# Lightning attention with a top-8 router on one core: seven block products for the keys, queries and gates of two batches, SiLU and tanh on ScalarE, a new order of work

## The chip, the core and the metric

One core of one Trainium2 chip runs the whole kernel, and it is the only program there. The metric is the device time of one execution in microseconds (us), lower is better.

## The reference, cut to what matters

```
x: (B=4, N=512, H=512) f32; 16 heads of 128; blocks of 64 tokens
xn   = layernorm(x)
qkv  = silu(xn @ w_qkv.T)                 # per head q, k, v of 128 each
per head, blocks scanned in order of time, kv starts at 0:
    o  = (q * q_decay) @ kv + ((q @ k.T) * diag_decay) @ v
    kv = block_decay * kv + (k * k_decay).T @ v
out  = norm_w * rms_norm(o over all 2048 columns)
gate = sigmoid(xn @ w_gate.T)
s    = (gate * out) @ w_out.T
logits = xn @ router_weight.T + router_bias      # 64 experts
scores = softmax(logits); top 8 per token
ffn  = xn * sum(top scores) + sum(top scores * expert_bias rows)
return x + s * silu(ffn)
```

## The kernel before, in words

Five engines work from five instruction lists. `Lane.do` and `Lane.dma` (L65, L74) append to the list of one engine, in the order in which the Python code runs, and an engine plays its list strictly in that order, waiting for semaphores where it must (`play`, L84). All DMAs go through the list of one engine, SyncE (`sp`), so a DMA that waits holds back all DMAs behind it. Buffers are handed out in turn by small rings (`Ring`, L100): `ring` for four PSUM banks `psR`, `tring` for the scratch rows `T`, `xring` for six rows `xs`, `rring` for two buffers `raw` of weights.

Products are computed in fp32r with each operand split in a high and a low part: ScalarE copies the high part (`xh`, `wh`, `qh`, ...), VectorE subtracts it to get the low part (`xl`, `wl`, `ql`, ...), and three matmuls (high x high, high x low, low x high) stand for one product.

Work goes in steps of one pair of heads and one batch, 32 of them (`order`), batches 0 and 1 through all eight pairs, then batches 2 and 3 back through the pairs; each step has two heads, so there are 64 units u. For each unit:

- `project` (L311) computes keys, then queries, then gates, each as one group of 12 matmuls of 512 columns (four parts of the inner 512, times three) into a bank of `psR`. `silu` (L329) takes the sigmoid on ScalarE and multiplies on VectorE, and splits the result. `gate` (L475) takes a sigmoid on ScalarE.
- `values` (L349) computes the values of both heads for two tiles of tokens, 24 matmuls of 256 columns, twice a step.
- `scores` (L369) transposes the keys and multiplies keys with queries; `decayed` (L385) weighs them with a table `D` of decays (loaded from `dtab`, which the kernel builds in DRAM at the start); `state` (L416) makes the key-value state after the first half of the tokens, and `mix` (L427) sums the head's output in `psO`.
- `gated` (L445) multiplies `psO`, norm weights and gates, splits the result into `zh`, `zl`, squares `psO` on ScalarE and adds the squares on GpSimd into `ss`.
- `project_out` (L518), once a step, multiplies by the output weights, four tiles of six matmuls, and VectorE adds each tile to `yacc`.

`split_piece` (L286) prepares the weights, each a copy on ScalarE and a subtraction on VectorE. The router (L591 to L668) is spread over the units by a table of due times (`later`, `hook`). At the start, the tiles of `x` are normalised (`moments`, `spread`, `normalise`) in a staggered order, so that VectorE works on one tile while GpSimd takes the root for another, then transposed (`turn`) and split (`place`). At the end, `fetch` (L524) has loaded the rows of all last tiles before they are needed (into `xs`, `raw` and `D`), and `finish_tile`, `scale_tile` and `finish_scaled_tile` scale, multiply and store them, part of it on ScalarE and GpSimd.

Of the kernel before, what the change touches and what calls it, by code (L numbers as in the profile page):

```python
# [13 lines left out]
P = 128  # L14
# [6 lines left out]
NX = 6  # L21
TAKEN = -3e38
# [6 lines left out]
QK = (QK0, QK1)  # L29

# [82 lines left out]
def build(nc, x, w, slope, norm_w, rw, rb, eb, ident_in, steps_in, out):  # L113
    gscr = nc.dram_tensor("gscr", (B * N, H), F32, kind="Internal").ap()
    dscr = nc.dram_tensor("dscr", (NH, ROW), F32, kind="Internal").ap()
    dtab = nc.dram_tensor("dtab", (NH, P, N), F32, kind="Internal").ap()

    with ExitStack() as ctx:
# [7 lines left out]
        xh, xl = sb("xh", [P, 3, KT, N], F32R), sb("xl", [P, 3, KT, N], F32R)  # L126
        wh, wl = sb("wh", [P, 5, 1024], F32R), sb("wl", [P, 5, 1024], F32R)
        vh, vl = sb("vh", [P, 3, 256], F32R), sb("vl", [P, 3, 256], F32R)
        qh, ql = sb("qh", [P, N], F32R), sb("ql", [P, N], F32R)
        kh, kl = sb("kh", [P, 2, P], F32R), sb("kl", [P, 2, P], F32R)  # L130
        ph, pl = sb("ph", [P, 2, C], F32R), sb("pl", [P, 2, C], F32R)
        dh, dl = sb("dh", [P, C], F32R), sb("dl", [P, C], F32R)
        kvh, kvl = sb("kvh", [P, P], F32R), sb("kvl", [P, P], F32R)
        zh, zl = sb("zh", [P, 2, N], F32R), sb("zl", [P, 2, N], F32R)
        rhl = sb("rhl", [P, KT, 2 * E], F32R)
# [3 lines left out]
        qf, kf, vf = sb("qf", [P, N]), sb("kf", [P, N]), sb("vf", [P, 3, 512])  # L139
# [3 lines left out]
        T = sb("T", [P, 4, N])  # L143
        D = sb("D", [P, 2, 2, N])
        sg = sb("sg", [P, 2, N])
        yacc = sb("yacc", [P, 2, 4, H])
        ss = sb("ss", [P, 2, N])
        sq = sb("sq", [P, 2, N])
# [28 lines left out]
        psR = ctx.enter_context(nc.psum_tensor("psR", [P, 4, 512], F32))  # L177
# [14 lines left out]
        ring = Ring(4)  # L192
        tring = Ring(4)
        xring = Ring(NX)
        rring = Ring(2)
        sqring = Ring(2)
# [4 lines left out]
        def mm(o, l, r, start, stop):  # L201
            return lambda e: e.matmul(o, l, r, start=start, stop=stop)  # L202

        def group(o, ops, after, then={}):

            for i, (l, r) in enumerate(ops):
                ev = pe.do(mm(o, l, r, i == 0, i == len(ops) - 1), *(after if i == 0 else ()), *then.get(i, ()),
                           mark=i == len(ops) - 1)
            return ev


        ln_ev = {}
# [5 lines left out]
        def moments(tt, i, ld):  # L218
            return dve.do(lambda v: v.bn_stats(st[:, tt % 4, :], xs[:, i, :]), ld)

        def spread(tt, e):
# [4 lines left out]

        def stat(tt, i, ld):
            spread(tt, moments(tt, i, ld))

        def normalise(tt, i, ld):  # L230
            return dve.do(lambda v: v.tensor_scalar(xs[:, i, :], xs[:, i, :], mv[:, tt, 0:1], rstd[:, tt:tt + 1],
                                                    ALU.subtract, ALU.mult), ld, ln_ev[tt])

        x_ready, x_hi, x_used = {}, {}, {}

        def turn(i, nx, in_psO=False):
            bank, free = (None, o_free[0]) if in_psO else ring.take()
            dst = psO if in_psO else psR[:, bank, :]
            for k in range(KT):
                ev = pe.do(lambda e, k=k: e.transpose(dst[:, k * P:(k + 1) * P], xs[:, i, k * P:(k + 1) * P],  # L240
                                                      ident[:, :]), *((nx, ident_ev) + free if k == 0 else ()),
                           mark=k == KT - 1)
            xring.give(i, ev)
            return bank, ev

        def place(tt, bank, ev, slot, prev_use=None):
            t = tt % 4
            src = (psO[:, :] if bank is None else psR[:, bank, :]).rearrange("p (k t) -> p k t", k=KT)
            dh, dl = xh[:, slot, :, t * P:(t + 1) * P], xl[:, slot, :, t * P:(t + 1) * P]
            hi = act.do(lambda a: a.activation(dh, src, ACT.Copy), ev, prev_use)  # L250
            lo = dve.do(lambda v: v.tensor_sub(dl, src, f32(dh)), hi)  # L251
            if bank is None:
                o_free[0] = (lo,)
            else:
                ring.give(bank, lo)
            x_ready[slot] = x_ready[(slot, t)] = lo
            x_hi[(slot, t)] = hi

        def xpose(tt, i, nx, slot, prev_use=None):
            place(tt, *turn(i, nx), slot, prev_use)  # L260


        seq = list(range(PAIRS)) + list(range(PAIRS - 2, -1, -1))
        to_load = [(0, p) for p in (VV, QK0, GG, QK1, OO)]
        to_load += [(wi, p) for wi in range(1, len(seq)) for p in (VV, QK0, GG, QK1, OO)]
        w_ready, w_hi, w_used, loaded = {}, {}, {}, {}

        def load_piece():
            if to_load:
                wi, piece = to_load.pop(0)  # L270
                i, free = rring.take()
                loaded[(wi, piece)] = i, sp.dma(raw_port[i], raw[:, i, :], w[seq[wi], piece], *free)

        def split_half(wi, piece, c):

            i, ld = loaded[(wi, piece)]
            cs = slice(c * 512, c * 512 + 512)
            w_hi[(piece, c)] = hi = act.do(lambda e: e.activation(wh[:, piece, cs], raw[:, i, cs], ACT.Copy),  # L278
# [3 lines left out]
            if c == 1:  # L282
                rring.give(i, lo)
                load_piece()
# [689 lines left out]
```

How the kernel before makes its waits and increments, by code:

```python
    def play(self, eng):  # L84
        for waits, make, inc in self.queue:
            for sem, v in waits:
                eng.wait_ge(sem, v)
            ins = make(eng)
            if inc:
                ins.then_inc(*inc)
# [836 lines left out]
            @block.sync  # L927
            def _(e):
                sp.play(e)
                for port in xs_port + [dscr_port]:
                    e.wait_ge(port.sem, port.count)
                for lane, v, _ in ends:
                    e.wait_ge(lane.sem, v)
```

## Time and profile before

| | |
|---|---|
| time, median of 2 runs | 1157.47 us (1156.66 to 1158.28) |
| span of the profiled execution | 1155.8 us |
| the profiled runs' time around that span | 1.7 us (median less span) |
| TensorE busy | 1139.6 us, 99% |
| VectorE busy | 782.3 us, 68% |
| ScalarE busy | 521.8 us, 45% |
| GpSimd busy | 103.4 us, 9% |

The page shows one profiled execution. The last row of the table of engines that matters for the result is that of TensorE. Busy matmuls overlap in the records: what one matmul costs is read from the time between two starts, not from its mean duration.

### The profile page before, as it was taken

The numbers are of one execution on the slowest core, as the hardware profiler recorded it, in microseconds if no ns is written. First come the engines' busy times: TensorE is split into PE (matmuls) and PEld (weight loads), VectorE is DVE, ScalarE is ACT, GpSimd is POOL, SyncE is SP. The second block draws the span as 40 slices with busy tenths as digits, with TensorE's granted clock in tenths as the row PEclk, the third lists the DMA queues.
The fourth block names the chain that finished last, engine by engine and source line by source line (L and its number), as shares of the span: only waits on it lengthen the run. The fifth ranks groups of instructions, "written<-read, shape, count | busy, mean of one in ns | idle before, by whom it ended". The sixth has DMA issues, their size and how long they took to land.

```text
span 1155.8 us, 16461 instructions
## 1 busy us (share of the span) xinstructions
PE 1139.6 (99%) x6668; PEld 1005.5 (87%) x6668; DVE 782.3 (68%) x1504; ACT 521.8 (45%) x1132; POOL 103.4 (9%) x97
## 2 busy tenths in 40 slices
PE   8899999999999999999999999999999999999997
PEld 6788888888888888888988888888888888888885
DVE  7565676766767778657576777667676676665557
ACT  4444454444544444544334444445444454444442
POOL 4000000000010001000100000000000000000012
PEclk9899999999999999999999999999999999999999
DMA  5621122112122121111222122112111221111303
GB/s 163 206 69 37 38 64 74 55 46 73 38 73 64 56 83 64 47 55 57 72 71 94 55 67 71 46 51 69 64 46 47 73 64 56 46 37 57 126 19 110
DMA packets 34044, 78.12 MB, mean 68 GB/s; under 512 B 3744, under 2 KB 8112, under 8 KB 33968
## 3 DMA queue, kind: packets, MB, share of 16 engines
q1 hardware_dynamic: 33968, 77.07, 20.3%
q8 instruction: 52, 0.85, 0.3%
q14 instruction: 24, 0.20, 0.1%
HBM read 68.64 MB, written 12.61 MB: 70 GB/s over the span
## 4 chain that ended last, share of the span: by engine, by line
PE 96%; DMA 2%; DVE 1%; ACT 0%; SPq 0%; issue 0%; POOL 0%; DVEq 0%; ACTq 0%
PE psR L202 76%; PE psS L202 9%; PE psO L202 9%; PE psS L373 1%; DMA dtab<-dscr 1%; PE psR L240 0%; DMA xs<-x 0%; DMA D<-dtab 0%; DMA dscr<-dval 0%; DVE wl L281 0%; DVE xl L251 0%; DVE yacc L584 0%; SPq L76 0%; PE psR L608 0%; PE psR L648 0%; DVE yacc L560 0%
## 5 line engine op out<-in xcount | busy, mean ns | idle before, releaser
L332 ACT ACTIVATE T<-psR 128x512 f32<-128x512 f32 x192 | 114.4, 596 | 291.1 <-PE psR L202 290.7
L202 PE MATMUL psR<-xh,wh 128*128 128x512 f32 x768 | 220.1, 408 | 0.4 <-DVE wl L281 0.4
L202 PE MATMUL psR<-xl,wh 128*128 128x512 f32 x768 | 206.6, 391 | 0.0
L202 PE MATMUL psR<-xh,wl 128*128 128x512 f32 x768 | 205.9, 390 | 0.0
L202 PEld LDWEIGHTS psR<-xl,wh 128*128 128x128 f32 x768 | 144.7, 188 | 31.9
L202 PEld LDWEIGHTS psR<-xh,wl 128*128 128x128 f32 x768 | 144.2, 188 | 31.4
L471 POOL TENSOR_TENSOR ss<-ss,sq 128x512 f32<-128x512 f32 x59 | 76.3, 1293 | 860.7 <-ACT sq L463 860.7
L202 PEld LDWEIGHTS psR<-xh,wh 128*128 128x128 f32 x768 | 134.6, 190 | 20.6 <-DVE wl L281 0.6
L281 DVE TENSOR_TENSOR wl<-raw,wh 128x512 fp32r<-128x512 f32 x150 | 114.6, 804 | 32.8 <-ACT wh L278 32.6
L333 DVE TENSOR_TENSOR qf<-psR,T 128x512 f32<-128x512 f32 x64 | 44.3, 692 | 113.8 <-ACT T L332 113.7
L514 DVE TENSOR_TENSOR yacc<-psR,yacc 128x512 f32<-128x512 f32 x109 | 73.1, 689 | 41.5 <-PE psR L202 41.5
L202 PE MATMUL psR<-wh,zh 128*128 128x512 f32 x256 | 100.0, 391 | 0.3 <-DVE zl L454 0.3
L202 PE MATMUL psR<-wh,zl 128*128 128x512 f32 x256 | 99.6, 389 | 0.0
L202 PE MATMUL psR<-wl,zh 128*128 128x512 f32 x256 | 99.6, 389 | 0.0
L333 DVE TENSOR_TENSOR vf<-psR,T 128x512 f32<-128x512 f32 x64 | 43.8, 686 | 71.9 <-ACT T L332 71.9
L278 ACT ACTIVATE wh<-raw 128x512 fp32r<-128x512 f32 x150 | 85.7, 622 | 8.6 <-DMA raw<-w 8.6
L202 PE MATMUL psR<-wh,xh 128*128 128x256 f32 x512 | 83.9, 286 | 0.0
L202 PE MATMUL psR<-wh,xl 128*128 128x256 f32 x512 | 82.5, 283 | 0.0
L202 PE MATMUL psR<-wl,xh 128*128 128x256 f32 x512 | 82.4, 283 | 0.0
L202 PEld LDWEIGHTS psR<-wh,xl 128*128 128x128 f32 x512 | 70.8, 192 | 0.0
L202 PEld LDWEIGHTS psR<-wl,xh 128*128 128x128 f32 x512 | 70.8, 192 | 0.0
L202 PEld LDWEIGHTS psR<-wh,xh 128*128 128x128 f32 x512 | 70.4, 191 | 0.0
(141 smaller groups left out, 1941.8 us busy)
## 6 DMA issues: line engine op xcount, KB each, us to landing
raw<-w SPq DMA_DIRECT2D x75, 512.0 KB, 3.6
xs<-x SPq DMA_DIRECT2D x45, 256.0 KB, 3.9
D<-dtab SPq DMA_DIRECT2D x15, 512.0 KB, 4.8
gscr<-xs SPq DMA_DIRECT2D x16, 256.0 KB, 2.0
out_dram<-yacc SPq DMA_DIRECT2D x16, 256.0 KB, 2.0
dtab<-dscr SPq DMA_DIRECT2D x2, 1792.0 KB
xs<-gscr SPq DMA_DIRECT2D x13, 256.0 KB, 3.9
dtab<-dscr SPq DMA_DIRECT2D x2, 256.0 KB
```

The source lines that it names most:

```text
L202: return lambda e: e.matmul(o, l, r, start=start, stop=stop)
L278: w_hi[(piece, c)] = hi = act.do(lambda e: e.activation(wh[:, piece, cs], raw[:, i, cs], ACT.Copy), ld, w_used.get(piece))
L281: lambda e: e.tensor_sub(wl[:, piece, cs], raw[:, i, cs], f32(wh[:, piece, cs])), hi)
L332: e = act.do(lambda a: a.activation(T[:, t, :], psR[:, bank, :], ACT.Sigmoid), ev, *free)
L333: e = dve.do(lambda v: v.tensor_mul(dst, psR[:, bank, :], T[:, t, :]), e)
L373: turned = pe.do(lambda e, t=t: e.transpose(psS[:, 1024 + t * P:1024 + t * P + P], kf[:, t * P:t * P + P], ident[:, :]), *((ready["k"], *k ...
L471: a = lane.do(lambda g: g.tensor_add(ss[:, y, :], ss[:, y, :], sq[:, j, :]), q, ss_ev.get(y))
L514: e = dve.do(lambda v: v.tensor_add(acc, psR[:, bank, :], acc), ev, y_ev.get((y, t)))
```

## The change

Two batches are now computed together. For a pair of batches and one head, keys and queries (or the gates of two heads) are a product of a 2 x 2 block matrix of weights (rows: the two outputs, columns: the two halves of the inner 512) with a 2 x 2 block matrix of activations (rows: halves, columns: the two batches). Eight block products of 6 matmuls (two parts of 256, times three) were needed; `seven` does it with seven, over sums and differences of blocks (`FACTORS`), seven of weights and seven of activations.

- `combine` builds the sums of activations on GpSimd (four subtractions of 256 columns per pair of token tiles); `tile_a` and `tile_b` transpose 14 blocks for two tiles, where 8 were.
- `weights` builds the sums of weights on GpSimd (four operations of 256 columns per piece) and splits seven blocks in four steps; `value_weights` splits six blocks after one GpSimd sum of 512 columns; weights are prepared anew for each of 16 pairs (15 before).
- The results are shared through PSUM: product 1 is copied by ScalarE from its bank to the bank `psB` (`seed`), product 5 by ScalarE to `T` (`s5`), and VectorE adds after product 6 (`u2`) and after product 7 (`c22`). Product 6 waits for `seed`, products 7 and 3 for `u2`, product 4 for `c22`.
- SiLU is one ScalarE instruction (`Silu`), the VectorE products are gone. The gates are `Tanh` of half the input; `gated` adds 1, and half the norm weight is put in by the split. The router takes its exponentials from `Silu`.
- `psR` has three banks (four before), `T` five rows.
- The work of a pair v is ordered by hand: `first_keys`, `heads`, `second_keys`, `gates` (for the next pair), with `opening` and `closing` at either end of each pair of batches. Deferred splits (`owed`, `settle`) are gone. At the start both batches are normalised one tile at a time. At the end, a plain loop fetches and finishes the last eight tiles.

```diff
+ORDER = (1, 5, 6, 2, 7, 3, 4)
+FACTORS = {1: (0, 0), 5: (1, 4), 6: (2, 5), 2: (3, 1), 7: (4, 3), 3: (5, 2), 4: (6, 6)}
...
+        def combine(t, a, na, b, nb):
...
+            e1 = pool.do(lambda g: g.tensor_sub(c1[:, lo], xb[:, lo], xa[:, lo]), na, nb, *ifree)
+            e3 = pool.do(lambda g: g.tensor_sub(c2[:, lo], xb[:, lo], xb[:, hi]), nb, *jfree)
+            e2 = pool.do(lambda g: g.tensor_sub(c1[:, hi], xb[:, hi], c1[:, lo]), e1)
+            e4 = pool.do(lambda g: g.tensor_sub(c2[:, hi], xa[:, hi], c1[:, hi]), e2)
...
+        def product(n, dst, start, after):
+            iw, ix = FACTORS[n]
+            ks = [slice(k * P, (k + 1) * P) for k in range(2)]
+            ops = [(gh[:, iw, ks[k]], xh[:, ix, k, :]) for k in range(2)]
+            ops += [(gh[:, iw, ks[k]], xl[:, ix, k, :]) for k in range(2)]
+            ops += [(gl[:, iw, ks[k]], xh[:, ix, k, :]) for k in range(2)]
...
+        def seven(kind, nx):
...
+            def p6():
+                ev = product(6, psB[:, :], False, (s["seed"],))
+                e, s5 = psR[:, s["e"], :], T[:, s["t5"], :]
+                s["u2"] = dve.do(lambda v: v.tensor_add(e, psB[:, :], s5), ev, s["s5"])
+                next(nx, None)
...
+            def p7():
+                ev = product(7, psB[:, :], False, (s["u2"],))
+                t, free = tring.take()
+                s5 = T[:, s["t5"], :]
+                s["c22"] = dve.do(lambda v: v.tensor_add(T[:, t, :], psB[:, :], s5), ev, *free)
...
+            def p4():
+                ev = product(4, psB[:, :], False, (s["c22"],))
...
+        for t in range(4):
+            normal(t)
+            tile_a(t, rows_of[t][0], norm[t])
+            if t == 1:
+                all_steps(value_weights(0))
         e = pool.do(lambda g: g.tensor_scalar(dexp[:, :], dexp[:, :], sl[:, :], None, ALU.mult), sl_ev, dexp_ev)
         dval_ev = pool.do(lambda g: g.tensor_tensor(dval[:, :], ebase[:, :], dexp[:, :], ALU.pow), e, ebase_ev)
...
+        def second_keys(v, nx, ow):
+            p1, p5, p6, p2, p7, p3, p4 = seven(QK1, nx)
+            p1()
+            p5()
+            next(ow)
+            p6()
+            p2()
+            p7()
+            next(ow)
+            p3()
+            split_keys(0)
+            p4()
+            split_queries(0)
+
+        def gates(v, nx):
+            p1, p5, p6, p2, p7, p3, p4 = seven(GG, nx)
+            p1()
+            p5()
+            p6()
+            do_scores(v, 2)
+            p2()
+            split_keys(1)
+            p7()
+            split_queries(1)
+            do_state(v, 2)
+            p3()
+            do_mix(v, 2)
+            p4()
+            split_values(1, 1)
...
+        values(0)
+        for t in range(4):
+            normal(4 + t)
+            combine(t, rows_of[t][0], norm[t], rows_of[4 + t][0], norm[4 + t])
+            tile_b(t, rows_of[t][0], rows_of[4 + t][0], norm[4 + t])
...
+            if t == 1:
+                half_values(1, 0)
+                all_steps(weights(QK0, 0))
+        half_values(1, 1)
...
+        opening(0)
+        for v in range(1, 7):
+            steady(v)
+        closing(7, second_rows())
+        values(0)
+        values(1)
+        split_values(0, 0)
+        opening(8)
+        for v in range(9, 15):
+            steady(v)
+        closing(15, nothing())
+        for tt in range(8, 16):
+            fetch(tt)
+            finish_tile(tt // 4 % 2, tt)
```

`finish_tile` is two VectorE operations on a tile and a DMA of it to the output; `fetch` is two loads, of `x` and of `gscr`; `normal(t)` is `stat` (statistics on VectorE, the root on GpSimd) and `normalise`. `steady(v)` is `heads` (which begins with `first_keys`), `second_keys`, `gates`. `closing(15, nothing())` has, after the second keys, scores, state and mix of two units with little between them, and both output products.

## Rows read from the trace of the kernel before

**Rows 1.** The page: busy time of the engines.

```profile
PE 1139.6 (99%) x6668; PEld 1005.5 (87%) x6668; DVE 782.3 (68%) x1504; ACT 521.8 (45%) x1132; POOL 103.4 (9%) x97
```

**Rows 2.** Waits of TensorE (us in total, times, longest us), and two stretches: us, busy by engine, granted clock, DMA.

```profile
PE psS L202 <- ACT kt L392: 5.4, 1, 5.4
...
100.00:600.00 500.00, 500.00 (x2944) 443.07 (x2943) 344.07 (x673) 228.54 (x498) 41.62 (x37) 1.00 0.18 60
```

**Rows 3.** The chain that ended last, one piece of it.

```profile
486.64 10.93 PE psR L202 x48
```

**Rows 4.** The costliest groups: busy us, mean ns.

```profile
L202 PE MATMUL psR<-xh,wh 128*128 128x512 f32 x768 | 220.1, 408 | 0.4 <-DVE wl L281 0.4
...
L471 POOL TENSOR_TENSOR ss<-ss,sq 128x512 f32<-128x512 f32 x59 | 76.3, 1293 | 860.7 <-ACT sq L463 860.7
...
L281 DVE TENSOR_TENSOR wl<-raw,wh 128x512 fp32r<-128x512 f32 x150 | 114.6, 804 | 32.8 <-ACT wh L278 32.6
...
L333 DVE TENSOR_TENSOR qf<-psR,T 128x512 f32<-128x512 f32 x64 | 44.3, 692 | 113.8 <-ACT T L332 113.7
...
L278 ACT ACTIVATE wh<-raw 128x512 fp32r<-128x512 f32 x150 | 85.7, 622 | 8.6 <-DMA raw<-w 8.6
```

**Rows 5.** Timeline of a steady stretch, TensorE, ScalarE and VectorE: start us, duration us.

```profile
511.83 0.60 PE L202 MATMUL psS<-vf,kt 128*128 128x128 f32 x4
...
512.03 0.60 ACT L332 ACTIVATE T<-psR 128x512 f32<-128x512 f32 x1 [1.31 <-PE psR L202]
...
512.65 0.69 DVE L333 TENSOR_TENSOR kf<-psR,T 128x512 f32<-128x512 f32 x1 [1.96 <-ACT T L332]
```

**Rows 6.** One operation of VectorE: duration ns least, median, most.

```profile
L281 DVE TENSOR_TENSOR wl<-raw,wh x150: 676/685/1374, 10.3 to 1107.3; 128x512 fp32r<-128x512 f32 x150
```

**Rows 7.** Timeline of the start.

```profile
3.53 1.31 DVE L219 BATCH_NORM_STATS2 st<-xs 128x6 f32<-128x512 f32 x2 [2.15 <-DMA xs<-x]
...
7.12 0.56 POOL L224 TENSOR_TENSOR rstd<-ve,mhalf 128x1 f32<-128x1 f32 x1 [1.36 <-DVE ve L223]
...
7.56 0.53 DVE L231 TENSOR_SCALAR xs<-xs,mv,rstd 128x512 f32<-128x512 f32 x1
...
9.87 0.99 PE L240 MATMUL psR<-ident,xs 128*128 128x128 f32 x4 [0.33 <-DVE xs L231]
...
10.20 5.78 POOL L715 TENSOR_TENSOR dval<-ebase,dexp 128x33 f32<-128x33 f32 x1
...
36.85 1.22 PE L202 MATMUL psS<-vf,kt 128*128 128x128 f32 x4 [5.44 <-ACT kt L392]
37.73 2.05 PE L202 MATMUL psR<-xh,wh 128*128 128x512 f32 x4
...
41.95 1.07 PE L202 MATMUL psR<-xh,wh 128*128 128x512 f32 x4
```

**Rows 8.** DMA issues in 1129 to 1130.9 us: KB each, us to landing.

```profile
out_dram<-yacc SPq DMA_DIRECT2D x1, 256.0 KB, 2.0
xs<-x SPq DMA_DIRECT2D x1, 256.0 KB, 2.9
xs<-gscr SPq DMA_DIRECT2D x1, 256.0 KB, 3.2
```

**Rows 9.** Timeline of the end.

```profile
1130.28 0.43 SPq L76 DMA_DIRECT2D xs<-x  x1
...
1148.46 0.39 PE L202 MATMUL psR<-wh,zl 128*128 128x512 f32 x1
...
1151.09 1.40 DVE L584 SCALAR_TENSOR_TENSOR yacc<-yacc,ro,xs 128x512 f32<-128x512 f32 x2
```

**Rows 10.** Groups of ScalarE and VectorE: a table load, and the two operations that finish a tile.

```profile
L676 ACT ACT_TABLE_LOAD x1 | 1.3, 1283 | 0.7 <-PEq L967 0.7
...
L560 DVE TENSOR_TENSOR yacc<-yacc,xs 128x512 f32<-128x512 f32 x11 | 8.6, 779 | 0.4
...
L558 DVE SCALAR_TENSOR_TENSOR yacc<-yacc,ro,xs 128x512 f32<-128x512 f32 x11 | 8.2, 745 | 1.1 <-POOL ro L492 1.1
```

More of the change, by code:

```diff
@@ L236, in turn @@
[L236 to L244, printed above, removed]
@@ new lines, in tokens @@
+        def tokens(blk, tiles=range(4)):
+            return [xr[(blk // 2, t)] for t in tiles]
+        steady = [p for v in range(1, 7) for p in ((GG, v), (QK0, v), (QK1, v), (VV, v), (OO, v))]
+        first = [(VV, 0), (QK0, 0), (GG, 0), (QK1, 0), (OO, 0)]
+        sequence = []
+        for r in range(2):
+            sequence += [(p, v + 8 * r) for p, v in first + steady]
+            sequence += [(p, 7 + 8 * r) for p in (GG, QK0, QK1, VV, OO)]
+        to_load, loaded = list(sequence), {}
@@ L792, in split_router @@
             j, ld = held.pop("e")
[L793 to L794 removed]
+            e_ready = split(eh[:, :], el[:, :], xs[:, j, :], ld)
             xring.give(j, e_ready)
[L797 to L803 removed]
@@ new lines, in build, with do_scores, do_state, do_mix @@
+        nw_ev = pool.do(lambda g: g.tensor_scalar(nw[:, :], nw[:, :], 0.5, None, ALU.mult), nw_ev)
+        unit = {}
+        def do_scores(v, i):
+            hh, j = divmod(i, 2)
+            k = 2 * v + hh
+            unit[(v, i)] = decayed(k, j, scores(j))
+            if j == 1:
+                load_decay(k + 2)
+        def do_state(v, i):
+            state(*divmod(i, 2), unit[(v, i)])
+        def do_mix(v, i, last=False):
+            hh, j = divmod(i, 2)
+            ev = mix(hh, j, unit.pop((v, i)))
+            gated(hh, j, 2 * (v % 8) + hh, ev, v % 8 == 0 and hh == 0, last)
@@ new lines, in second_rows, with get, put @@
+        def second_rows():
+            for t in range(4):
+                rows_of[8 + t] = None
+            pairs = {}
+            def get(t):
+                pairs[t] = load_rows(8 + t), load_rows(12 + t)
+            def put(t):
+                (a, lda), (b, ldb) = pairs.pop(t)
+                combine(t, a, lda, b, ldb)
+                tile_a(t, a, lda)
+                tile_b(t, a, b, ldb)
+            get(0)
+            all_steps(value_weights(8))
+            yield
+            get(1)
+            put(0)
+            yield
+            all_steps(weights(QK0, 8))
+            get(2)
+            put(1)
+            yield
+            get(3)
+            put(2)
+            yield
+            put(3)
+            yield
```

1032 lines of the change are left out of this document (561 added, 471 removed).

## The prediction

> **What bounds the kernel now.** I read the busy times first: TensorE is at 99%, VectorE at 68%, ScalarE at 45% [rows 1]. A busy matmul row overlaps its neighbours, so that alone proves little. The waits do: in the whole span TensorE's one wait of note is 5.4 us for `kt` at the start, and between 100 and 600 us it is busy for all of 500.00 us at full clock [rows 2]. The kernel is one unbroken stream of matmuls between a start and an end. What one costs is read from the chain: 48 matmuls of 512 columns in 10.93 us, 0.228 each, though their rows say 408 ns [rows 3, 4]. So a matmul left out is worth 0.228 us as long as nothing else becomes late, and a wait that TensorE did not have is paid in full.
>
> **The stream.** Keys, queries and gates are 2304 matmuls of 512 columns (three rows of 768, one of them in [rows 4]): 144 for each of 16 pairs with two batches. With seven products of 6 for eight it is 126, and 2016 in all: 288 x 0.228 = 65.6 us less. Values, scores, state, mix and output stay as they are. Transposes go from 4 blocks per tile to 14 per two tiles, 112 for 64; four small matmuls take at most 0.60 us [rows 5], and less in a stream, so 48 more are about 5 us, bounded by 0 (beside idle time at the start) and 7. Net **-60.5**.
>
> **Busy time of the others.** VectorE loses 192 SiLU products, 132 us by their rows' means (one of them [rows 4]), and gains 96 additions for `u2` and `c22` (66 us) and more weight splits: 48 x (0.42 + 3 x 0.69), with 0.42 as my estimate for half the columns, + 16 x 5 x 0.69 = 175 us against 150 x 0.69 = 103 (0.69 is the median of [rows 6]). With small items it stays near 780. But GpSimd gains 192 sums of 256 columns, 16 of 512 and 32 for x; with half of 1.29 us for a short one [rows 4] that is 125 + 21 + 21 us on top of 103. The subtraction `wl`, both inputs in SBUF, takes 685 ns as a rule and 1374 at worst, and its mean is 804 [rows 4, 6]: it is the worse when GpSimd adds. That is 18 us now; for GpSimd at 270 us I take 50 more, between 0 (they never meet) and 90 (VectorE spends a third of the time in such operations). ScalarE gains 96 copies (58 us) and splits (161 for 93), near 650. VectorE at some 830 and ScalarE at 650 of 1200 bound nothing by themselves. What counts is how late they are when TensorE asks.
>
> **The new waits.** From the end of a group to ScalarE's start is 0.20 us, its operation takes 0.60, VectorE starts 20 ns later and takes 0.69 [rows 5]. A link (product, one operation, product) is thus 0.8 to 0.9, and with the load of weights behind the wait about 1.0 to 1.1 us. What covers it is one product of 6, 1.37 us. The slack of 0.3 us is less than one operation queued in front. I follow a steady pair in program order, with 0.5 to 0.6 us for each operation in a queue:
> - second keys, `seed`: ScalarE first has `zh`, the square, and the split of values left by the mix before. It is done some 0.4 us late.
> - second keys, `u2`: a subtraction for the output weights stands in front on VectorE and meets GpSimd's sums. 0.4 late.
> - gates, `seed`: four copies of the second keys are in front. 0.2 late.
> - gates, mix: `kvl` needs `kvh`, and in front of that on ScalarE stand the result of `c22` (which waits for VectorE behind the decays) and `qh`. The first part of the mix covers 1.1. 1.2 late.
> - first keys, `u2`: behind the five operations of `decayed`. 0.3 late.
>
> Output tiles and values in `heads` cover all that is due there. Sum 2.5 us a pair, bounds 0 (the queues run ahead) and 6 (each of nine links one operation late). For 12 steady pairs **+30**, for the two openings **+8**.
>
> **The turn and the last units.** After pair 7 the second keys end, then the query split is needed at once (result, copy, subtraction: 2.1 us after the last product), the mix of unit 2 waits for scores, decays and two splits (5 us for 5 of work), and unit 3 the same, while 14 transposes per tile pass three banks whose release hangs on VectorE. I count 15 us of idle TensorE, bounds 5 and 25: **+15**. After pair 15 there is no filler, but fewer operations in the queues: 2.1 + 2.4 + 0.6 + 2.2 = **+7**.
>
> **The start.** Before, TensorE runs undisturbed from 41.95 us [rows 7], and until then it has done 48 matmuls of 256 columns, 72 of 512, small ones and 16 transposes, about 23 us of stream: 19 us are lost. After, VectorE's list has per tile: statistics 0.69 and two short ones, the root on GpSimd 0.56, normalise 0.53, transposes 0.99, ScalarE 0.60, subtraction 0.69 [rows 4, 6, 7]; with the hand-overs 4.6 us, one after the other, where before the tiles were staggered. From 3.5 us, with 2 for the value weights, four tiles end at 24. Then GpSimd's list has the power for the decays, 5.78 us [rows 7], in front of the next root: fifth tile normalised at 28.7. Each tile of the second batch takes 7.1 (2.1 for VectorE and root, GpSimd's four sums 2.6, three transposes, copies and subtractions), and 3 for the key weights: 57. With the last values the products begin at 61, after 18 us of stream: 43 lost, **+24**, bounds 10 and 35. The clock is in this: after its 5.4 us of idleness the first four matmuls took 2.05 us where they take 1.07 [rows 7].
>
> **The end.** Before, the last matmul starts at 1148.46, and the span ends 6.9 us after its end [rows 9], since all loads were issued long before. After, the loop puts into SyncE's list: loads of tile 8, store of tile 8 (waits for VectorE), loads of tile 9, and so on; no load can pass the store in front. Per tile: issue of the store and two loads (starts 0.4 to 0.5 apart), the landing of the second 3.2 after its issue [rows 8, 9], 0.75 and 0.69 on VectorE [rows 10]: 0.9 + 3.2 + 1.4 = 5.5 us. The first tile is ready 2.3 after the last matmul, seven more follow, the last store lands after 2.0: 2.3 + 38.5 + 2.0 = 43 for 7, **+36**. Bounds 25 (landing 2.0 only) and 40.
>
> **Sum.** 1155.8 - 60.5 + 30 + 8 + 15 + 7 + 24 + 36 = 1215.3 us of span, with 1.7 around it **1217 us**, 5% slower.
>
> **Rivals.**
> 1. *The links are covered and the stream stays unbroken.* ScalarE had gaps of 1.31 us and VectorE of 1.96 in the steady stretch [rows 5], and in program order their lists may run ahead. Then the 38 us of pairs and openings fall away and 10 of the turn: 1169, within 2% of before, thus not slower. It decides where a pair loses less than 0.4 us (with 1.0 it would be 1184). Against it: the slack of 0.3 us by the numbers above, and lists that put other work in front. Chance 0.14.
> 2. *VectorE as the bound.* GpSimd's sums come right beside the subtractions of the same piece, so they meet more often than by chance; each doubled one stands in front of a link. At 6 us a pair: 1217 + 14 x 3.5 = 1266. For it: 1374 ns [rows 6]. Against: a third of the time only. Chance 0.12.
> 3. *Table loads.* Before there is one, of 1283 ns [rows 10], since all functions lie in one table. If `Silu` and `Tanh` don't, ScalarE goes to and fro twice a pair (keys, gates), four times in an opening, 32 in all: 41 us, near a link each time: 1258. Nothing in this trace shows either function. Chance 0.08. The Trainium skill (ScalarE: Activation LUTs, Table sets: the hidden batching unit) says that functions are loaded as named sets and a switch costs the load and a drain, some 2.66 us; 32 of these would be 85 us and the time 1302. It lists tanh in two sets as a filler and does not list SiLU; the trace's 1283 ns agrees with its figure for the load alone.
> 4. *The ends are cheap too.* If the loads of the last loop get out ahead (they can't by the list) and the start is 10 us better, with rival 1: 1169 - 36 - 10 = 1123, faster. Chance 0.04.
>
> **How the numbers follow.** The forecast has 0.62, with its own range 1190 to 1245. The range that holds 8 in 10 takes in rival 1 and most of 2 and 3: 1168 to 1262. A measurement of this kernel tells about 2% from no change, so same ends at 1181. Faster is rival 4, 0.04; same is rival 1 and the forecast's thin lower edge, 0.16; slower the rest, 0.80.
>
> **What would show it.** Right: TensorE waits for ScalarE's and VectorE's results in every pair, most of all before the products 6 and 7 and in the mix of the gates; VectorE's busy share near 70%, GpSimd's over 20%; `wl`'s successor `gl` well over 0.69 us in the mean; the first product of keys near 61 us; eight stores 5.5 us apart after the last matmul; one table load. Wrong: TensorE busy without gaps in the middle (rival 1), table loads between keys and gates (rival 3), stores at the end closer than 4 us, or 288 matmuls less giving other than 0.228 each.

## The result and the profile after

The changed kernel took 1320.85 us in the median of 2 runs (1320.17 to 1321.53), the kernel before 1157.47: a ratio of 1.141, 95% interval 1.137 to 1.144. It is 14% slower, where 5% was forecast, and above the range. The span of the profiled execution is 1318.4 us.

The busy times, against [rows 1]:

```profile
PE 1142.0 (87%) x6422; PEld 971.1 (74%) x6422; DVE 854.2 (65%) x1527; ACT 637.3 (48%) x1364; POOL 311.2 (24%) x337
```

The records have 246 matmuls less, and TensorE's share falls from 99% to 87%. No other engine has become full. ScalarE's table load stayed the only one, against the same row in [rows 10]:

```profile
L831 ACT ACT_TABLE_LOAD x1 | 1.3, 1283 | 0.7 <-PEq L1238 0.7
```

The waits of TensorE (what is waited for: us in total, times, longest), where [rows 2] had one of 5.4:

```profile
PE psR L215 <- DVE yacc L684: 20.9, 21, 2.3
PE psR L269 <- POOL xs L291: 18.8, 8, 8.6
PE psB L215 <- DVE psR L477: 16.7, 7, 5.1
PE psO L215 <- DVE kvl L601: 16.4, 16, 2.7
PE psR L269 <- DVE yacc L259: 13.6, 3, 5.4
PE psR L269 <- DVE xs L259: 13.1, 3, 6.2
PE psB L215 <- ACT psB L442: 6.8, 4, 3.0
PE psR L215 <- DVE yacc L682: 5.4, 4, 1.5
```

L684 and L682 are VectorE's addition and copy of output tiles, which give banks back; L291 is GpSimd's `combine`; L477 is `u2`; L601 is `kvl`, the low part of the key-value state, which the mix needs; L442 is the seed; the two L259 are the normalisation at the start.

For a table by stage I count, for each matmul, its start to the next start at the full rate (0.227 us for 512 columns, 0.1195 for 256, 0.113 for 128 and 0.100 for one). That sum is the stream; what the gaps between starts have beyond it is lost. All figures of this table are worked out so from the records of the profiled executions. "Start" is until the first product of keys, "tail" from the start of the last matmul to the end of the span.

| us | stream | first product | lost in start | lost after it | tail | span |
|---|---|---|---|---|---|---|
| before | 1128.2 | 18.1 | 7.8 | 11.3 | 7.3 | 1155.8 |
| after | 1066.8 | 66.7 | 46.1 | 161.9 | 42.2 | 1318.4 |
| e_eight_b | 1126.8 | 55.2 | 37.3 | 58.0 | 41.8 | 1265.2 |
| e_nosums | 1066.8 | 64.3 | 43.7 | 127.7 | 42.6 | 1282.2 |
| e_start | 1066.8 | 51.9 | 31.3 | 163.4 | 42.3 | 1305.1 |
| e_tail | 1066.8 | 66.0 | 45.4 | 156.4 | 19.2 | 1289.2 |
| e_all7 | 1066.8 | 52.0 | 31.4 | 140.9 | 19.6 | 1260.1 |
| e_all7ns | 1066.8 | 47.3 | 26.7 | 120.0 | 19.8 | 1234.6 |
| e_all8 | 1126.8 | 33.4 | 15.5 | 50.3 | 19.0 | 1212.9 |

The stream fell by 61.4 us, start and tail grew by some 38 and 35, and the loss after the first product grew by 151. The windows of the changed kernel show where (us, busy by engine, granted clock, DMA), against [rows 2]:

```profile
66.70:128.00 61.30, 57.09 (x290) 47.70 (x289) 37.73 (x69) 39.83 (x85) 16.03 (x20) 0.97 0.39 117
128.00:560.00 432.00, 399.44 (x2288) 341.16 (x2287) 301.12 (x552) 224.30 (x485) 98.87 (x102) 0.99 0.20 60
560.00:750.00 190.00, 159.02 (x872) 134.67 (x871) 120.88 (x202) 84.45 (x179) 50.55 (x57) 0.91 0.25 84
750.00:1210.00 460.00, 432.80 (x2466) 370.34 (x2465) 314.47 (x566) 248.36 (x536) 106.88 (x108) 0.99 0.17 53
```

By my count these four stages lose 7.0, 50.0, 48.2 and 46.2 us. The steady pairs, six in the second stage and six in the fourth, lose 8 us each, and the turn between them 48. Before, TensorE was busy for every one of 500 us. After, VectorE is busy for 301 of 432 us in the steady pairs (70%) and still comes too late. This stretch shows how (timeline, VectorE and GpSimd, then TensorE; start, duration), against [rows 5]:

```profile
429.93 1.39 POOL L646 TENSOR_TENSOR ss<-ss,sq 128x512 f32<-128x512 f32 x1 [6.21 <-ACT sq L636]
430.19 1.41 DVE L335 TENSOR_TENSOR kl<-kf,kh 128x256 fp32r<-128x256 f32 x1
431.27 1.48 POOL L378 TENSOR_TENSOR wt<-raw 128x512 f32<-128x512 f32 x1
431.52 1.78 DVE L335 TENSOR_TENSOR gl<-raw,gh 128x512 fp32r<-128x512 f32 x1
433.23 0.68 DVE L335 TENSOR_TENSOR ql<-qf,qh 128x512 fp32r<-128x512 f32 x1
433.83 0.68 DVE L684 TENSOR_TENSOR yacc<-psR,yacc 128x512 f32<-128x512 f32 x1
434.43 0.68 DVE L335 TENSOR_TENSOR wvl<-raw,wvh 128x512 fp32r<-128x512 f32 x1
...
432.70 0.39 PE L215 MATMUL psR<-woh,zl 128*128 128x512 f32 x1
434.56 0.50 PE L215 MATMUL psR<-woh,zh 128*128 128x512 f32 x1 [1.47 <-DVE yacc L684]
```

`kl` takes 1.41 us for 256 columns, where the shortest of that size takes 0.41 (the group of `gl` below), and `gl` 1.78. Each ends shortly after the GpSimd operation beside it. Behind them in VectorE's list stands the addition that gives a bank of `psR` back, and TensorE, out of three banks, waits 1.47 us for it. The groups of the subtractions say the same, against `wl` in [rows 4, 6] (tile and group views; ns least, median, most, then us and mean ns):

```profile
L335 DVE TENSOR_TENSOR gl<-raw,gh x144: 406/692/1787, 46.6 to 1210.6; 128x512 fp32r<-128x512 f32 x96, 128x256 fp32r<-128x256 f32 x48
...
L646 POOL TENSOR_TENSOR ss<-ss,sq 128x512 f32<-128x512 f32 x60 | 82.5, 1376 | 623.9 <-ACT sq L636 623.9
```

The most is 1787 ns (before 1374), and GpSimd's own addition is longer too, 1376 against 1293.

The start, against [rows 7] (GpSimd's power in front of the next root, a wait of TensorE for the seventh tile, the first product of keys):

```profile
23.43 5.70 POOL L929 TENSOR_TENSOR dval<-ebase,dexp 128x33 f32<-128x33 f32 x1
...
29.34 0.58 POOL L254 TENSOR_TENSOR rstd<-ve,mhalf 128x1 f32<-128x1 f32 x1
...
51.89 0.69 PE L269 MATMUL psR<-ident,xs 128*128 128x128 f32 x2 [6.23 <-DVE xs L259]
...
66.71 0.63 PE L215 MATMUL psR<-xh,gh 128*128 128x512 f32 x2
```

The end, against [rows 9] (VectorE and SyncE's queue):

```profile
1278.06 0.34 SPq L82 DMA_DIRECT2D out_dram<-yacc  x1
1278.45 0.43 SPq L82 DMA_DIRECT2D xs<-x  x1
1278.92 0.45 SPq L82 DMA_DIRECT2D xs<-gscr  x1
1281.83 0.75 DVE L709 SCALAR_TENSOR_TENSOR yacc<-yacc,ro,xs 128x512 f32<-128x512 f32 x1 [3.80 <-DMA xs<-gscr]
...
1283.34 0.34 SPq L82 DMA_DIRECT2D out_dram<-yacc  x1
```

From store to store it is 5.28 us here and 5.4 later (1288.75, 1294.19), as forecast: no load gets past the store in front of it.

### The profile page after: what moved, and what is told of

Read it like the earlier page. It is cut to its first block, busy times and chain, and to the rows that moved or that the text cites. A ratio compares the mean times of both kernels' runs of the same rounds, so it can differ in the third digit from the quotient of the medians.

```text
span 1318.4 us, 16636 instructions
## 1 busy us (share of the span) xinstructions
PE 1142.0 (87%) x6422; PEld 971.1 (74%) x6422; DVE 854.2 (65%) x1527; ACT 637.3 (48%) x1364; POOL 311.2 (24%) x337
## 4 chain that ended last, share of the span: by engine, by line
PE 51%; DVE 26%; ACT 14%; issue 3%; POOL 3%; DMA 2%; SPq 1%; POOLq 0%; DVEq 0%
PE psR L215 31%; PE psB L215 10%; PE psS L215 5%; DVE gl L335 5%; PE psO L215 4%; ACT gh L334 2%; ACT zh L635 2%; DVE T L630 2%; DVE kl L335 2%; DMA xs<-gscr 2%; DVE T L577 2%; ACT sg L449 2%; DVE ql L335 1%; DVE T L585 1%; DVE yacc L684 1%
## 5 line engine op out<-in xcount | busy, mean ns | idle before, releaser
L646 POOL TENSOR_TENSOR ss<-ss,sq 128x512 f32<-128x512 f32 x60 | 82.5, 1376 | 623.9 <-ACT sq L636 623.9
L335 DVE TENSOR_TENSOR gl<-raw,gh 128x256 fp32r<-128x256 f32 x144 | 107.9, 750 | 51.5 <-ACT gh L334 51.4
L215 PE MATMUL psR<-xh,gh 128*128 128x512 f32 x384 | 125.6, 408 | 0.0
L215 PE MATMUL psR<-woh,zh 128*128 128x512 f32 x256 | 106.7, 417 | 21.3 <-DVE yacc L684 15.0
L215 PE MATMUL psR<-xl,gh 128*128 128x512 f32 x384 | 120.5, 396 | 0.0
L215 PE MATMUL psB<-xh,gh 128*128 128x512 f32 x288 | 97.8, 421 | 25.7 <-DVE psR L477 16.7
L215 PE MATMUL psR<-xh,gl 128*128 128x512 f32 x384 | 118.9, 391 | 0.0
L215 PE MATMUL psR<-woh,zl 128*128 128x512 f32 x256 | 102.3, 400 | 0.0
L215 PE MATMUL psR<-wol,zh 128*128 128x512 f32 x256 | 102.3, 399 | 0.0
L684 DVE TENSOR_TENSOR yacc<-psR,yacc 128x512 f32<-128x512 f32 x112 | 75.4, 683 | 27.5 <-PE psR L215 27.3
L215 PE MATMUL psB<-xl,gh 128*128 128x512 f32 x288 | 91.8, 401 | 0.0
L215 PE MATMUL psB<-xh,gl 128*128 128x512 f32 x288 | 91.7, 400 | 0.0
L215 PEld LDWEIGHTS psB<-xh,gh 128*128 128x128 f32 x288 | 47.3, 190 | 49.3 <-DVE psR L477 27.6
L630 DVE SCALAR_TENSOR_TENSOR T<-sg,psO 128x512 f32<-128x512 f32 x64 | 43.7, 684 | 57.7 <-PE psO L215 57.7
```

The source lines that it names most:

```text
L215: return lambda e: e.matmul(o, l, r, start=start, stop=stop, skip_group_check=shared)
L335: return dve.do(lambda v: v.tensor_sub(dl_, src, f32(dh_)), hi)
L630: z = dve.do(lambda v: v.scalar_tensor_tensor(T[:, t, :], sg[:, k, :], 1.0, psO[:, :], ALU.add, ALU.mult), ev, sg_ready, *free)
L646: a = lane.do(lambda g: g.tensor_add(ss[:, j, :], ss[:, j, :], sq[:, :]), q, ss_ev.get(j))
L684: e = dve.do(lambda v: v.tensor_add(acc, src, acc), ev, y_ev.get((j, t)))
```

## The experiments

In these texts "after" and "before" are the two kernels, and the kernel before was timed beside each (1156.9 to 1158.2 us). Most versions ran once. How far one run can be trusted is seen in e_tail below: its code is that of the changed kernel up to the last loop, and yet it is some 6 us ahead when it gets there. Differences of that size say nothing.

**The order without the seven products.** e_eight keeps the new order, start, end and three banks, and has eight products over the plain blocks, no sums:

```diff
-            e1 = pool.do(lambda g: g.tensor_sub(c1[:, lo], xb[:, lo], xa[:, lo]), na, nb, *ifree)
...
+            def output(n):
+                ops = [(gh[:, iw, ks[k]], xh[:, ix, k, :]) for iw, ix, k in pairs]
...
+                ev = group(psR[:, bank, :], ops, (g_ready[i], *tokens(2 * j), *free), True, True)
```

> The order of work of the changed kernel with eight block products in place of seven: keys, queries and gates of two batches as four groups of 12 matmuls, no sums of weights or activations on GpSimd, no seed, s5, u2, c22. The stream grows by 288 x 0.228 = 65.6 us less 48 transposes (5 us). Theory A (what the middle of the kernel loses is the price of the seven products, their links and GpSimd's sums): some 80 us or more of TensorE's waits go, and the time is 1300 us or less. Rival B (the order of the lists is to blame, whatever the products): nearly all waits stay, 1365 to 1380 us.

Measured: 1282.98 us (1 run). In this version the second batch's keys are written before the scores of a unit have read the old ones, so those scores are of other keys. TensorE also waits for these keys, 16 times, 11.0 us in all. In e_eight_b the keys come after the scores:

```diff
             def p5():
-                output(1)
+                pass
 
             def p6():
+                output(1)
                 next(nx, None)
```

> Eight products in the changed order as in e_eight, with the keys of the second batch computed after the scores that still read the old ones. The same work in the same places: 1280 to 1286 us.

Measured: 1267.04 us (1 run), 13 below what I expected, as those waits are gone; 109.5 above the kernel before, with as many matmuls for keys, queries and gates. The order is not alone in this: the serial start, the plain last loop and the missing fourth bank are in it too (e_all8 below mends them in part). By the table: 34.5 in the tail, 46.7 after the first product, 29.5 in the start (of the loss that the kernel before has after its first product, most lies before 42 us). The seven products come on top with 53.8 us, though they save 60 of stream: their price is 114.

**GpSimd's weight sums left out.** The factors of weights are then plain blocks; it leaves the sums of the weights out of the computation:

```diff
-                e1 = pool.do(lambda g: g.tensor_add(s1, a21, a22), ld, *wt2_free[0])
-                e2 = pool.do(lambda g: g.tensor_sub(s2, s1, a11), e1)
-                e3 = pool.do(lambda g: g.tensor_sub(a21, a21, a11), e2)
-                return e2, e3
+                return ld, ld
```

> Seven products as changed, but GpSimd's sums of weights are left out (208 operations, the blocks of weights are then not the right ones); all matmuls, links, copies and subtractions stay. Theory A1 (GpSimd's sums double VectorE's subtractions of two SBUF inputs, VectorE falls behind, and output tiles and u2 are late): the mean of the weight subtractions falls from 750 to below 620 ns, waits of the output tiles for yacc nearly vanish, 30 to 50 us less, 1270 to 1290. Rival A2 (the links themselves and what the lists put in front): under 15 us less, 1305 or more.

Measured: 1283.99 us (1 run), 37 less. TensorE's waits for the additions of output tiles (L684 above) fall from 20.9 to 9.8 us. Is that the wait for the sums, or what they do to VectorE? e_dummy leaves the sums out too, and has GpSimd make as many additions on a buffer that nobody reads:

```diff
+                for k in range(3):
+                    chain[0] = pool.do(lambda g: g.tensor_add(s1, s1, s2), ld if k == 0 else None, chain[0])
+                return ld, ld
```

> As the run without GpSimd's sums of weights, but with GpSimd additions of the same number and size at the same places that nobody waits for (they add a scratch row to itself; the blocks of weights are again not the right ones). Nothing depends on them, they only take GpSimd's and VectorE's common way to SBUF. Contention theory: most of the 37 us that the sums cost comes back, 1308 to 1320 us, and the weight subtractions are again 700 to 750 ns in the mean. Dependency theory (the splits wait for the sums, or the sums for the splits): it stays at 1284 to 1290.

Measured: 1314.14 us (1 run). 30 of the 37 us are back, with nobody waiting for these additions. The groups of full-width `gl` of e_nosums, then of e_dummy:

```profile
L335 DVE TENSOR_TENSOR gl<-raw,gh 128x512 fp32r<-128x512 f32 x144 | 102.9, 717 | 79.3 <-ACT gh L334 79.2
```

```profile
L335 DVE TENSOR_TENSOR gl<-raw,gh 128x512 fp32r<-128x512 f32 x144 | 116.8, 813 | 81.3 <-ACT gh L334 81.2
```

So the price of the sums is mostly contention; the other 7 us are about what two runs of the same code differ by. The 96 ns in the mean of these 144 operations are 14 us of VectorE. Other operations of VectorE with both inputs in SBUF are longer too: `T<-qf,D` (64 of 256 columns) goes from 433 to 576 ns, `vl` (64 of 256) from 663 to 781. In all VectorE's busy time goes from 813.9 to 849.6 us, 36 more, and the kernel pays 30: though VectorE is busy for only 65% of the time, most of its extra work reaches the kernel's time.

**Moving a wait.** Most of the waits for `u2` stood behind a router step in front of the second keys. e_hook5 moves that step ahead by an output tile:

```diff
-            do_out(v - 1, 1, between({1: (v, 4)}, None, None, None, None))
+            do_out(v - 1, 1, between({1: (v, 4), 3: (v, 5)}, None, None, None, None))
...
-            hook(v, 5)
```

> The router's step that stood right before the second keys goes into the last output tile, before the mix. Where a router tile was normalised and scaled on VectorE at that place, product 7 of the second keys waited 2.4 to 3.1 us for u2. Theory A2: these waits go, 12 to 16 us less, 1305 to 1309. If VectorE is late anyway (A1), the wait moves to the output tiles or the mix, and under 5 us are won.

Measured: 1311.86 us (1 run), 9 less, between the two expectations and little more than the 6 us of chance. The waits for `u2` fell from 16.7 to 4.6 us, and part of it came back at the seeds (4 waits of 6.8 us in the changed kernel, now the row below):

```profile
PE psB L215 <- ACT psB L442: 13.1, 8, 2.9
```

e_state gives the state in the gates more time ahead of the mix, which waits for `kvl`:

```diff
             p2()
+            do_state(v, 2)
             split_keys(1)
             p7()
             split_queries(1)
-            do_state(v, 2)
```

> In the gates the state is computed right after product 2, so that kvh stands before kh, the result of c22 and qh in ScalarE's list, and kvl before kl and c22 on VectorE. The mix of unit 2 waited for kvl 14 times for 1.2 us. If this is the lists' order (A2), the waits for kvl go and 12 to 17 us are won, 1304 to 1309. If the time is only passed on (c22 gets later by 0.3 to 0.6 us and product 4 waits), under 6 us.

Measured: 1321.28 us (1 run), no gain. The waits for `kvl` fell from 16.4 to 1.2 us, and those for `u2` doubled from 16.7:

```profile
PE psB L215 <- DVE psR L477: 33.6, 21, 4.8
```

Here the wait that was given more cover moved to the next link. It fits that VectorE and ScalarE are behind and that TensorE's wait was where they caught up; e_hook5, where only part of the wait came back, shows that it need not be all.

**Banks.** e_bank4 puts the accumulator of products 6, 7 and 4 in one ring of four banks with the rest. The work is the same; where a transposition used the bank last, products 6 and 7 overwrite part of it instead of adding, so part of the sums differs:

```diff
-        ring = Ring(3)
+        ring = Ring(4)
...
+                s["b"], bfree = ring.take()
+                s["B"] = psR[:, s["b"], :]
```

> The changed kernel with psB taken from one ring of four banks, so that output tiles, values and the router have four banks while no seven products run. TensorE waited some 33 us for VectorE to empty one of three banks (18.0 of output tiles alone). Theory A2 (a missing buffer): 15 to 30 us less, 1291 to 1306. Rival (VectorE is behind at the end of the first keys, and the wait only moves to the scores or the mix): under 8 us less.

Measured: 1296.51 us (1 run), 24 less. Output tiles and values have a bank more to run into. TensorE's waits for the additions of output tiles fell from 20.9 to 8.6 us, those for the seeds rose from 6.8 to 9.4, and waits for `wvl` came (10.3 us). The loss after the first product is 139.9 us by the count of the table, against 161.9.

**The end.** e_tail fetches three tiles ahead:

```diff
-        for tt in range(8, 16):
+        for tt in range(8, 11):
             fetch(tt)
+        for tt in range(8, 16):
             finish_tile(tt // 4 % 2, tt)
+            if tt + 3 < 16:
+                fetch(tt + 3)
```

> The last loop with the loads of three tiles issued ahead of the first store, and each further load right behind a store, so two tiles ahead. The tail after the last matmul was 42 us with seven turns of 5.5. If it is the order of SyncE's list, a turn falls to the 1.4 us of VectorE or 1.4 of issuing, the tail to 14 to 20 us, and the time to 1295 to 1300; nothing else changes. If loads were slow for another reason, it stays above 30.

Measured: 1290.98 us (1 run), 30 less, more than I expected: 23 are in the tail. The other 6 lie ahead of the loop, where nothing was changed, and are chance. Two stores of it (1.4 us apart early on, where they were 5.3):

```profile
1271.83 0.34 SPq L82 DMA_DIRECT2D out_dram<-yacc  x1
...
1273.22 0.40 SPq L82 DMA_DIRECT2D out_dram<-yacc  x1
```

**The start.** e_start takes statistics one to three tiles ahead of the normalisation, for all eight tiles, and puts the power behind the first `combine`:

```diff
-        for t in range(4):
-            normal(t)
-            tile_a(t, rows_of[t][0], norm[t])
+        stats(0)
+        stats(1)
+        norms(0)
+        stats(2)
+        norms(1)
+        tile_a(0, rows_of[0][0], norm[0])
...
```

> The start with statistics and normalising of all eight tiles staggered ahead of the transposes on VectorE's list, rows 6 and 7 loaded at once, and the power for the decays behind the first combine on GpSimd. The first product of the keys began at 66 us. If the serial list is the cause, it begins at 46 to 54 and 12 to 20 us are won, 1301 to 1309; if GpSimd's combine (2.6 us and more per tile) bounds the second batch alone, under 8.

Measured: 1307.14 us (1 run), 14 less, first product at 51.9 us, 15 earlier.

**SiLU and tanh alone.** e_silu is the kernel before, with these functions on ScalarE and nothing else of the change:

```diff
-            e = act.do(lambda a: a.activation(T[:, t, :], psR[:, bank, :], ACT.Sigmoid), ev, *free)
-            e = dve.do(lambda v: v.tensor_mul(dst, psR[:, bank, :], T[:, t, :]), e)
+            e = act.do(lambda a: a.activation(dst, psR[:, bank, :], ACT.Silu), ev, *used.get(slot, ()))
```

> The kernel before with one part of the change alone: SiLU as one ScalarE instruction without VectorE's product (192 of them gone), gates as tanh, the router's exponentials and gates from Silu. Stream-bound theory: TensorE's stream is untouched and never waited, so nothing is won or lost, 1155 to 1160 us, with VectorE's busy time down by some 130 us and one table load. If the tables had to be switched it would be 30 us or more slower.

Measured: 1161.47 us (5 runs), ratio 1.0032, interval 1.0019 to 1.0045. Busy times, and the window that [rows 2] had:

```profile
PE 1140.7 (98%) x6668; PEld 1006.9 (87%) x6668; DVE 665.7 (57%) x1296; ACT 518.0 (45%) x1132; POOL 103.5 (9%) x98
...
100.00:600.00 500.00, 500.00 (x2951) 443.43 (x2951) 294.05 (x582) 229.16 (x504) 42.22 (x38) 1.00 0.18 61
```

117 us of VectorE's work are gone and the time does not fall: TensorE was the bound. The 4 us more are lost in the start (11.6 against 7.8 by the count of the table), where I had put the halving of the norm weights into GpSimd's list: it runs at 10.16 us, and the first root, which stood at 5.20 before, comes behind it at 10.39.

**All repairs together**, with seven products (e_all7) and with eight (e_all8): start, tail and router step as above, and one output tile of four and half of the values go to `psB`, which serves as a fourth bank while no group of seven uses it:

```diff
+                if t == 1:
+                    bank, free, src = None, b_free[0], psB[:, :]
+                else:
+                    bank, free = ring.take()
```

> Seven products with four repairs at once: staggered start, loads ahead in the last loop, the router's step before the second keys moved, and psB as a fourth bank for one output tile in four and half of the values. Where the parts add up: 1320.8 less 30 (loads), 14 (start), 9 (router) and about 20 (bank), 1248 us, between 1238 and 1258. If one wait only gives way to the next (VectorE and ScalarE being behind), the bank and the router bring less than half together, 1262 or more. Slower than before in any case.

> The same four repairs with eight block products in place of seven. The eight products had fewer waits for banks (8 us) and little at the start from GpSimd; 1283 less 30, 8 to 14 and 5 to 10: 1230 to 1240 us. If the seven products cost more than they save even after the repairs, this is below the seven with repairs by 8 us or more; if their price was the missing bank and the serial start, it is above it.

Measured: e_all7 1262.3 us (4 runs), ratio 1.091 (1.089 to 1.0935); e_all8 1215.47 us (4 runs), ratio 1.0496 (1.048 to 1.051). e_all7 is just where I expected it if waits only give way to each other; e_all8 is 15 us better than expected. From the changed kernel the single parts give 14 + 30 + 9 + 24 = 77 us, the whole 59. Some 6 of the 77 are chance (e_tail), and the fourth bank is only a part of one here; the rest does not add up. In e_all7 the waits for the additions of output tiles are down from 20.9 to 4.8 us, and these lead (waits of TensorE):

```profile
PE psR L269 <- POOL xs L291: 27.1, 7, 8.6
PE psO L215 <- DVE kvl L605: 19.2, 17, 3.1
PE psB L215 <- ACT psB L442: 14.4, 8, 3.8
```

In the steady window of e_all8 the order costs little once it has part of a fourth bank: TensorE is busy for 424.34 of 432 us, with VectorE at 254 against 301:

```profile
128.00:560.00 432.00, 424.34 (x2471) 372.30 (x2470) 253.75 (x495) 197.85 (x430) 37.04 (x32) 1.00 0.20 63
```

**The sums, once more, in the repaired kernel.** e_all7ns is e_all7 with the edit of e_nosums; the weights' sums are left out.

> The repaired version with seven products (1262.3), with GpSimd's sums of weights left out (the sums of the activations stay), so the factors of keys, queries, gates and values are not the reference's. Theory A (the sums cost by slowing VectorE's subtractions, whose lateness reaches TensorE through whatever link is tight): the 37 us that they cost in the changed kernel come back here too, 1222 to 1232 us, close to the eight products' 1215.5; the waits of TensorE for u2 and the seeds shrink most, gl's mean is near 0.64 us. Theory B (the repairs have made room, so slower subtractions fall into slack): less than 15 us, 1248 or more, and the distance of 47 us between seven and eight products lies in the links of the seven products themselves.

Measured: 1237.34 us (2 runs), ratio 1.069 (1.066 to 1.072). It lies between the two theories: 25 us come back, not 37 and not under 15. Full-width `gl` is at 718 ns in the mean. Still it is 22 us above e_all8, with 60 us less of stream. So in the repaired kernel the seven products cost 107 us, against the 60 of stream that they save (60 + 47): 25 by the sums of weights and 82 by the links, the extra splits and the sums and transpositions of the activations. By the table 16 of these lie in the start (31.4 lost in e_all7, 15.5 in e_all8). How these 82 divide was not tried.

No version with the new order came below the kernel before.

## Why the prediction was wrong

The sign, the stream and the end held. The losses between the first product and the last did not: 60 us were forecast and 162 measured.

- **The stream**, -60.5: measured -61.4. Right.
- **The end**, 43 us behind the last matmul: 42.2. Right, and e_tail shows the cause. Mended, it gave 23 us.
- **The start**, first product at 61 with 43 lost: 66.7 and 46.1. Right to 6 us. e_start shows that the serial order is at least 14 of it.
- **Table loads** (rival 3): refuted, the one load of [rows 10] is still the only one. The Trainium skill (ScalarE: Activation LUTs, Table sets: the hidden batching unit) lists no SiLU; this trace shows it beside tanh without a second load. (The 2.66 us of the prediction are from the section What ACT_TABLE_LOAD costs of the same page; no run here shows a switch.)
- **The links** (2.5 us a pair): their sum is near the truth, in part by luck. Over the two steady windows (gaps that are more than 250 ns over the rate) `kvl` cost 15.6 us for 14.4 forecast, `u2` 12.5 for 8.4, the seeds 3.4 for 7.2. `kvl` came as foreseen, one wait a pair. `u2` did not: nearly all of its 12.5 us are five waits of 2 to 3 us, and e_hook5 shows that they stood behind a router step, which the forecast did not have at that place.
- **The failed step** is the sentence "Output tiles and values in `heads` cover all that is due there", and with it the sum of 2.5 us a pair, for which 8 were measured (96 for 30). In the same two windows output and router tiles of TensorE waited 30.8 us, 2.6 a pair, for banks behind VectorE's operations on output tiles. I had counted the output tiles as cover for the work due in `heads` and not as work with a link of its own: a tile of six matmuls needs a bank back every 1.37 us, VectorE's addition takes 0.68, and between two of them stand the splits that second keys and values need, one of them doubled by GpSimd. In the whole span the waits of L684, 20.9 us, fall to 8.6 with a fourth bank (e_bank4), to 4.8 with part of one and the other repairs (e_all7), and to 9.8 with three banks but without GpSimd's sums of weights (e_nosums).
- **A term that I did not have**: gaps too short for the list of waits. From the first product of keys to 1235 us, gaps less than 250 ns over the rate have 41 us of loss in the changed kernel, net, and some 15 in e_eight_b, where the kernel before has 4. In the steady pairs it is 27, 2.2 a pair. About half of the 41, 20 us, is the clock: these matmuls ran at the lower of its two levels. The other 21 are mostly slow starts of groups. Both are shown below.
- **The turn**, 15 and an opening of 4: 48 us from 560 to 750. 16.7 of it are four waits of transpositions for `combine`: GpSimd, at half the columns 0.73 us at best and 1.17 beside VectorE, makes four of them in a row for each pair of tiles. Another 9 are the lower clock, to which TensorE fell five times there. I had looked at the banks and not at GpSimd's list or the clock.

One wait of the turn (timeline, GpSimd, then TensorE):

```profile
644.93 1.17 POOL L290 TENSOR_TENSOR xs<-xs 128x256 f32<-128x256 f32 x1
...
646.05 1.17 POOL L291 TENSOR_TENSOR xs<-xs 128x256 f32<-128x256 f32 x1
...
647.28 2.23 PE L269 MATMUL psR<-ident,xs 128*128 128x128 f32 x8 [8.61 <-POOL xs L291]
```

Before these sums stood, in GpSimd's list, those of the next pair's weights, the last of which waits for a `gl`.

- **Rival 2**, VectorE as the bound, had the mechanism that was missing: GpSimd's operations doubling the subtraction in front of a link. It gave 6 us a pair and 1266. e_dummy shows 30 us from contention in the whole kernel. But it was not alone, and VectorE is at 65%, never full: lateness, not load. I gave it 0.12 and took the two as exclusive, where they add.

What would the forecast have been with the measured terms? In loss from the first product to the last matmul the forecast had 30 + 8 + 15 + 7 = 60 us, and 162 were measured. These 102 us are the whole error but one: the span was 103 us longer than forecast. Of the 102, 66 are in the steady pairs (banks 31, short gaps 27, the rest small) and most of the others in the turn.

## What to carry to other kernels

A kernel whose first engine runs without a gap has little to gain from fewer operations on it if the others must then answer inside one product. e_eight_b shows that the new order, start and end with three banks lost 110 us without any of the seven products, e_all8 that 58 are left of it with the start, the end and part of a fourth bank repaired, and e_silu that 117 us less of VectorE's work gained nothing. When you price links, walk every piece of the pair, also the pieces meant as filler: count for each the banks it needs back and what stands in front of the operation that frees them. A wait that is moved may only be passed on, as in e_state. And each wait can cost more than its own length, if the clock falls behind it.

## What the runs showed of the hardware

**Two engines, one port.** In the timeline above, `kl` (430.19, 1.41 us) ends 0.28 us after GpSimd's addition (429.93 + 1.39), `gl` (431.52, 1.78 us) 0.55 us after the next (431.27 + 1.48). The later one mostly stands still until the other is done. The Trainium skill (SBUF — State Buffer, Who interferes with whom) says that a VectorE instruction with two SBUF inputs contends with a GpSimd one that reads SBUF, and that the pair of ports that they share is an exclusive lock. This trace agrees: after GpSimd's end most of the 0.41 or 0.69 us is still to do. I had taken 1374 ns for the worst case, as before; with GpSimd at 24% it is 1787.

**After a wait the clock can fall.** One of the waits for `u2` (matmuls, then two windows: us, busy by engine, granted clock, DMA):

```profile
395.69 0.84 PE L215 MATMUL psB<-xh,gh 128*128 128x512 f32 x2 [2.74 <-DVE psR L477]
396.33 1.06 PE L215 MATMUL psB<-xl,gh 128*128 128x512 f32 x2
397.18 1.06 PE L215 MATMUL psB<-xh,gl 128*128 128x512 f32 x2
...
396.20:399.60 3.40, 3.40 (x9) 2.64 (x9) 1.05 (x2) 0.60 (x2) 0.95 (x1) 0.50 0.00 0
399.60:403.00 3.40, 3.40 (x16) 2.80 (x16) 1.86 (x4) 3.23 (x8) 0.00 (x0) 1.00 0.31 59
```

Behind the wait of 2.74 us the granted clock is 0.50, the lower level of 1.2 GHz, and two matmuls start 0.85 us after two others, where 0.454 is the rate at the full 2.4 GHz. TensorE is busy throughout all the same. Between the first product and 1235 us the changed kernel has 13 such stretches, 61 us long, and 140 matmuls in them lose 20 us beside the waits; in the kernel before such matmuls lose 1.3 us, in e_eight_b 7. The seven stretches in the steady pairs all begin within 2 us after a wait of 1.6 to 2.9 us. It is not every such wait: after one of 2.9 us at 472.3 the clock stays up. Before the first product 41 of 66.7 us are at the lower level.

**A group that begins after a wait starts slowly, even if the wait is short.** Product 6 in the gates (matmuls, weight loads, and the seed it waits for, start and duration):

```profile
478.79 0.61 PE L215 MATMUL psR<-xh,gl 128*128 128x512 f32 x2
479.25 0.73 PE L215 MATMUL psB<-xh,gh 128*128 128x512 f32 x2
479.82 0.63 PE L215 MATMUL psB<-xl,gh 128*128 128x512 f32 x2
...
478.56 0.41 PEld L215 LDWEIGHTS psR<-xh,gl 128*128 128x128 f32 x2
479.25 0.30 PEld L215 LDWEIGHTS psB<-xh,gh 128*128 128x128 f32 x2 [0.27 <-ACT psB L442]
...
478.61 0.59 ACT L442 ACTIVATE psB<-psR 128x512 f32<-128x512 f32 x1
```

The seed ends at 479.20, 0.05 us before the stream would need it, and no wait is listed for the matmul. But the weight load, which stood 0.23 us ahead of its matmul in the group before, now stands beside it, and the first two matmuls take 0.57 us from start to start where two take 0.46. The 0.11 us is lost here, at the full clock. At that clock, from the first product to 1235 us, 129 gaps are 90 to 250 ns over the rate, 16 us together; the kernel before has 11 and e_eight_b 49.

**VectorE's rows overlap as well.** 433.23, 433.83, 434.43: back to back these three operations start 0.60 us apart, though each row says 0.68.
